# Attention stage of a four-stage block: the next batch's queries transposed between the scores of heads 1 and 2, their squares taken before the output copy, and the low parts of the key/value and output weights computed on GpSimd

## The reference, cut to what matters

```
q, k, v = projections of x[b]                 # 32 query heads, 8 key/value heads, D = 128
q, k = rope(rmsnorm(q)), rope(rmsnorm(k))
k_all = concat(cached keys (512), new k (128));  v_all likewise      # pages by block table
scores = q @ k_all.T * D**-0.5, masked where cache position >= cache_seqlens[b]
probs = softmax(scores);  o = probs @ v_all
x = x + o.reshape(S, 32*D) @ Wo.T             # then dense, SwiGLU and adapter stages on x
```

## Time and profile before

| what | value |
|---|---|
| median of 3 runs | 1509.14 us (1508.47 to 1510.86) |
| profiled execution | 1509.87 us, its span 1508.1 us |
| TensorE busy | 1410.0 us, 93% of the span |
| VectorE, ScalarE, GpSimd busy | 1023.3, 849.9, 667.3 us |
| granted TensorE clock, mean | 0.988 |

### The profile page before, as it was taken

One profiled execution on the slowest core, in us unless ns is written; L12 is line 12 of the kernel. 1 busy time (PEld: TensorE's weight loads), 2 busy tenths in 40 slices (PEclk: granted clock), 3 DMA queues, 4 the chain that ended last, 5 costly groups with the idle time before them and its releaser, 6 DMA issues. The chain is left out here.

```text
span 1508.1 us, 25464 instructions
## 1 busy us (share of the span) xinstructions
PE 1410.0 (93%) x7864; PEld 1211.3 (80%) x7864; DVE 1023.3 (68%) x2128; ACT 849.9 (56%) x2191; POOL 667.3 (44%) x971
## 2 busy tenths in 40 slices
PE   3799999999999999999999999999999796999998
PEld 2678888888888888788888878888888576888886
DVE  7666777777777777776777677777777454545543
ACT  3555665566666656665665566656656445434444
POOL 5788644444544544455454444544444280010112
PEclk9999999999999999999999999999999998999999
DMA  5243235414611561344135414522120344443422
GB/s 184 105 138 126 62 105 158 110 43 140 187 36 47 159 185 28 92 146 139 45 100 155 118 43 140 173 51 56 35 58 7 119 155 141 148 150 112 168 98 98
DMA packets 185182, 164.41 MB, mean 109 GB/s; under 512 B 122608, under 2 KB 159344, under 8 KB 174832
## 3 DMA queue, kind: packets, MB, share of 16 engines
q1 hardware_dynamic: 178352, 127.60, 28.4%
q0 software_dynamic: 6720, 35.66, 7.2%
HBM read 131.77 MB, written 31.46 MB: 108 GB/s over the span
## 5 line engine op out<-in xcount | busy, mean ns | idle before, releaser
L469 ACT ACTIVATE at_pT_hi<-at_ps 128x512 fp32r<-128x512 f32 x320 | 180.0, 599 | 193.9 <-PE at_ps L852 192.2
L636 DVE TENSOR_TENSOR at_pT_lo<-at_ps,at_pT_hi 128x512 fp32r<-128x512 f32 x320 | 209.9, 685 | 110.2 <-ACT at_pT_hi L469 109.8
L401 POOL TENSOR_SCALAR at_probs<-at_probs,at_row_inv 128x640 f32<-128x640 f32 x256 | 209.6, 821 | 157.1 <-DVE at_row_inv L687 151.7
L681 DVE CUSTOM_DVE_ANT_0 at_scores<-at_ps,at_mask,at_inv_rms 128x640 f32<-128x640 f32 x256 | 223.6, 877 | 73.7 <-PE at_ps L65 66.7
L512 ACT ACTIVATE at_probs<-at_scores,at_neg_max 128x640 f32<-128x640 f32 x256 | 213.1, 833 | 53.8 <-DVE at_neg_max L681 51.4
L63 PE MATMUL at_ps<-at_kT_hi,at_qT_hi 128*128 128x320 f32 x512 | 166.2, 325 | 25.8 <-DVE at_neg_max L681 23.2
L852 PE MATMUL at_ps<-ident,at_probs 128*128 128x128 f32 x1280 | 160.8, 273 | 1.8 <-POOL at_probs L401 1.8
L64 PE MATMUL at_ps<-at_kT_lo,at_qT_hi 128*128 128x320 f32 x512 | 159.1, 311 | 0.0
L65 PE MATMUL at_ps<-at_kT_hi,at_qT_lo 128*128 128x320 f32 x512 | 159.0, 311 | 0.0
L852 PEld LDWEIGHTS at_ps<-ident,at_probs 128*128 128x128 f32 x1280 | 145.4, 141 | 12.7 <-POOL at_probs L401 3.2
L63 PE MATMUL at_ps<-at_pT_hi,at_v_hi 128*128 128x512 f32 x320 | 134.1, 419 | 6.8 <-DVE at_pT_lo L636 6.8
(11 more groups left out here) (217 smaller groups left out, 3549.0 us busy)
## 6 DMA issues: line engine op xcount, KB each, us to landing
kT_pages<-at_kv_stage SPq DMA_DIRECT2D x14, 1024.0 KB
v_pages<-at_kv_stage SPq DMA_DIRECT2D x14, 1024.0 KB
at_k_raw<-kT_pages SPq DMA_DIRECT2D x56, 256.0 KB, 4.9
at_v_raw<-v_pages SPq DMA_DIRECT2D x56, 256.0 KB, 3.8
sw_wgu_raw<-in_sw_gu SPq DMA_DIRECT2D x22, 512.0 KB, 3.4
staging<-in_L_cond_Wq SPq DMA_DIRECT2D x8, 1024.0 KB, 5.4
staging<-in_L_cond_Wo SPq DMA_DIRECT2D x8, 1024.0 KB
ds_mask_raw<-in_mask_Bx4096x_ik SPq DMA_DIRECT2D x8, 1024.0 KB, 4.9
```

What stands on the lines that cost most here:

```text
L401: pool.tensor_scalar(probs[:, h, :], probs[:, h, :], row_inv[:, h:h + 1], 1.0, ALU.mult, ALU.mult).then_inc(probs_done, 1)
L469: act.activation(out, src, ACT.Copy).then_inc(done, 1)
L636: dve.tensor_tensor(out, src, hi_part.bitcast(F32), ALU.subtract).then_inc(done, 1)
L681: dve.tensor_tensor_reduce(out=scores[h % 2][:], in0=slot(h), in1=mask[:, b, :], scale=inv_rms[b % 2][:, h:h + 1], scalar=3.0e38, op0=ALU. ...
```

## The change

1. TensorE issues the next item's `queries` after the scores of head 1 in place of after those of head 3; `late_kv` is gone, so every item has `project_kv` before the transposes of the probabilities.
2. ScalarE takes `squares` one item earlier: at the end of an item, for the next but one, ahead of the output copy. The squares of (0, 1) stand before the first item.
3. The lo parts of the key/value weights (two instructions of 128x512 per group) and, but for group 0, those of Wo (four per group) are computed by GpSimd. The key/value weights move from b = 7 to b = 6, and the slots move: three query groups after the next item's cached keys, the fourth after two probability transposes, the key/value groups (and the second half of Wo) after the last one. The semaphore `wqkv_done` is split into `wq_done` and `wkv_done`; the load of Wo waits for the first alone.

```diff
             groups = {0: {2: [0, 1], 3: [2, 3]}}
             if not last:
-                groups[B - 2] = {0: [0], 1: [1], 2: [2], 3: [3]}
-                groups[B - 1] = {0: [4], 1: [5]}
+                groups[B - 2] = {0: [0, 1, 2], 1: [3], 3: [4, 5]}
             return groups.get(b, {}).get(slot, [])
+
+        def split_apart(first, b, n):
+
+            return n >= DC if b else not first
...
                         wait_apart(sp, wo_done, g * WO_GROUPS + WO_GROUPS, sp_passed)
+                        wait_apart(sp, wkv_done, g * KV_GROUPS + KV_GROUPS, sp_passed)
                         load_qkv(g + 1)
...
                     if not last and b == B - 1:
-                        wait_apart(sp, wqkv_done, g * QKV_GROUPS + 2 * QKV_GROUPS, sp_passed)
+                        wait_apart(sp, wq_done, g * DC + 2 * DC, sp_passed)
                         load_wo(g + 1)
...
+            def qkv_group(g, n):
+                cs = slice(2 * (n - DC), 2 * (n - DC) + 2)
+                wait_apart(pool, wqkv_hi_done, g * QKV_GROUPS + n + 1, pool_passed)
+                pool.tensor_tensor(wkvT_lo[:, cs, :], wkv_raw[:, cs, :], wkvT_hi[:, cs, :].bitcast(F32), ALU.subtract).then_inc(wkv_done, 1)
+
+            def wo_group(g, n):
+                wait_apart(pool, wo_hi_done, g * WO_GROUPS + n + 1, pool_passed)
+                pool.tensor_tensor(woT_lo[:, n, :], wo_raw[:, n, :], woT_hi[:, n, :].bitcast(F32), ALU.subtract).then_inc(wo_done, 1)
...
                         key_scale(g1, b1)
+                    if b == 0 and not first:
+                        wo_group(g, 0)
+                    if more:
                         rotate_k(g1, b1)
                     if by_row:
                         gather(b2, range(2), k_rows, k_raw, k_loaded)
+                    if b == 0 and not first:
+                        wo_group(g, 1)
+                        wo_group(g, 2)
+                    if b == B - 2 and not last:
+                        qkv_group(g + 1, DC)
+                        qkv_group(g + 1, DC + 1)
                     if more2:
                         rotate_q(g2, b2)
+                    if b == 0 and not first:
+                        wo_group(g, 3)
...
-                    if more:
-                        squares(g1, b1)
-                    exps(g, b, 0)
-                    exps(g, b, 1)
-                    weights(0)
-                    exps(g, b, 2)
-                    exps(g, b, 3)
+                    for h in range(G):
+                        exps(g, b, h)
                     if more:
                         queries(g1, b1)
-                    weights(1)
-                    if more:
                         cached_keys(g1, b1)
+                    weights(0)
                     probs_T(g, b, 0)
                     probs_T(g, b, 1)
-                    weights(2)
+                    weights(1)
                     if more:
                         cached_values(g1, b1)
                         new_kv(g1, b1)
                     probs_T(g, b, 2)
+                    weights(2)
                     probs_T(g, b, 3)
+                    probs_T(g, b, 4)
                     weights(3)
-                    probs_T(g, b, 4)
                     if more:
                         new_keys(g1, b1)
+                    if more2:
+                        squares(*following(g1, b1))
                     hi(oT_hi[:], bank(O_BANK), pv_done, upto(g, b, KC, KC), oT_hi_done)
...
                         for n in weight_groups(b, slot, last):
-                            if b < 2:
-                                wo_group(g, n)
-                            else:
-                                qkv_group(g + 1, n)
+                            if not split_apart(first, b, n):
+                                if b < 2:
+                                    wo_group(g, n)
+                                else:
+                                    qkv_group(g + 1, n)
...
-                    late_kv = b == B - 1 and not last
-                    for h in range(G):
-                        score(g, b, h)
+                    score(g, b, 0)
+                    score(g, b, 1)
                     if more:
                         queries(g1, b1)
+                    score(g, b, 2)
+                    score(g, b, 3)
                     if not (first and b == 0):
                         output(g, b, range(G))
-                    if late_kv:
-                        project_ahead(range(2))
-                    elif more:
+                    if more:
                         project_kv(g1, b1)
...
-                    if late_kv:
-                        project_kv(g1, b1)
-                    else:
-                        project_ahead(range(2))
+                    project_ahead(range(2))
```

More of the change, by code:

```diff
@@ L190, in attention @@
         wqkv_hi_done = sem("wqkv_hi_done")
-        wqkv_done = sem("wqkv_done")
+        wq_done = sem("wq_done")
+        wkv_done = sem("wkv_done")
         wo_hi_done = sem("wo_hi_done")
@@ L240, in attention @@
         sp_passed = sem("sp_passed")
-        QKV_GROUPS, WO_GROUPS = DC + DC // 2, G
+        KV_GROUPS, WO_GROUPS = DC // 2, G
+        QKV_GROUPS = DC + KV_GROUPS
         def xT_raw(b):
@@ L290, in _ @@
                     load_qkv(0)
-            sp.wait_ge(wqkv_done, QKV_GROUPS)
+            sp.wait_ge(wq_done, DC)
             load_wo(0)
@@ L535, in _ @@
             new_keys(0, 0)
+            squares(0, 1)
             def group(g, last):
@@ L539, in group @@
                     g1, b1 = following(g, b)
-                    more = not (last and b == B - 1)
+                    more, more2 = not (last and b == B - 1), not (last and b >= B - 2)
                     def weights(slot):
@@ L644, in qkv_group @@
                 out, src, h = (t[:, n, :] if n < DC else t[:, cs, :] for t in ((wqT_lo, wq_raw, wqT_hi) if n < DC else (wkvT_lo, wkv_raw, wkvT_hi)))
-                lo(out, src, h, wqkv_hi_done, g * QKV_GROUPS + n + 1, wqkv_done)
+                lo(out, src, h, wqkv_hi_done, g * QKV_GROUPS + n + 1, wq_done if n < DC else wkv_done)
             def wo_group(g, n):
@@ L804, in project_q @@
                     if b == 0:
-                        pe.wait_ge(wqkv_done, g * QKV_GROUPS + c + 1)
+                        pe.wait_ge(wq_done, g * DC + c + 1)
                     ins = three_pass(pe, bank(Q_BANK), xT_hi[:, c, at], xT_lo[:, c, at], wqT_hi[:, c, :], wqT_lo[:, c, :], c == 0, c == DC - 1)
@@ L812, in project_kv @@
                 if b == 0:
-                    pe.wait_ge(wqkv_done, g * QKV_GROUPS + QKV_GROUPS)
+                    pe.wait_ge(wkv_done, g * KV_GROUPS + KV_GROUPS)
                 for c in range(DC):
```

## The result

The changed kernel takes 1471.94 us (median of 4 runs, 1471.15 to 1473.14), the kernel before on the same chip 1510.0 us: ratio 0.9748, 95% interval 0.9731 to 0.9765. The forecast was 1478, its range 1471 to 1490. The profiled execution has a span of 1470.7 us against 1508.1, 37.4 less, where the sum of the prediction gave 31.4.

The account below looks back on a forecast made before the run. TensorE, busy 1410.0 of 1508.1 us, was taken as the bound, so its waits count. Gains 20.6 + 2.5 + 14.7 less 6.4 of new waits gave 31.4 us, hence 1478 us, range 1471 to 1490.

Parts of the forecast that it names:

- the new waits: TensorE waiting for keys and queries delayed by GpSimd's lo parts: 6.4 us lost, 0.5 of it for groups 1 and 7.
- Queries into the gap: TensorE transposes the next queries while waiting to start head 2: 20.6 us gained in groups 1 to 6, 2.5 in group 7.
- the rival of the rotation as the bound: TensorE's moved query transposes wait for GpSimd's rotation in every item: 10 us of gain lost, 1488 us; chance 0.15.
- the gap move: Rival: TensorE reaches the probabilities 0.43 earlier and waits there; 23.1 us lost, 1501 us; chance 0.05.
- Squares: ScalarE's squares before the output copy: cost nothing, covered by its 0.36 wait; otherwise at most 0.3 to 0.5 per item.
- Weights: Items 6, 7 and 0 shed weight work and waits: 0.71, 0.40 and 0.99 each, seven times, 14.7 us gained.
- GpSimd's lo parts: Each 128x512 weight lo part on GpSimd takes 1.29 us, with 2841 ns the other end.
- the rival of a held GpSimd: VectorE holds up GpSimd's lo parts, 1.55 us more each: 54 us lost, 1532 us; slower 0.04, near break-even 0.02, less 0.02.
- the strictest reading of that rival: Each GpSimd lo part held by one VectorE lo part of some 0.7 us: 24 us lost, 1502 us.
- and the 1.06 of the jump stay: In b = 0, head 2's 1.06 us delay after the loop's jump remains; only 0.99 of that item's excess goes.
- the item starts late: In groups 2 to 6, item 0's late start makes GpSimd's lo parts cost 0.9 each: 4.5 us of new waits.
- Group 0: Items of the group with GpSimd's gathers: 0.43 won, about 0.7 lost to the late queries' rotation; counted as zero overall.

Follow-up runs that it names:

- padded: Changed kernel with 14 increments of a semaphore nobody waits for inside VectorE's loop, which then lies at 337-708: 1476.6 us.
- shifted: Changed kernel with 14 idle semaphore increments ahead of VectorE's loop, moving it unchanged in length from 337-694 to 351-708: 1474.7 us.
- squares late: Changed kernel with ScalarE's squares back at the item's start, all else as changed: 1492.0 us.
- weights alone: Changed kernel with queries again after head 3's scores and squares at the item's start; weight lo parts stay on GpSimd: 1495.1 us.
- order alone: Kernel before with only queries and squares moved as in the change; all lo parts stay on VectorE in their old places: 1490.6 us.
- placed repaired kernel: Changed kernel with group 0 ordered as before, GpSimd rotating queries one lo part earlier, and 14 idle increments ahead of ScalarE's loop: 1467.8 us.
- kernel before, shifted: Kernel before with fewer doubled semaphore waits on VectorE, moving its loop from 339-708 to 315-684: 1524.0 us.

## Why the prediction was right, and where its terms were off

The direction, the range and the main mechanism held. That the time lies inside the range, 0.9 above its lower end, is in part luck. The prediction gave 1471 to 1472 a chance of 0.03 and meant by it that the new waits would be absent. About half of them are there; the time came so low because a stall went that the sum let stay and no rival priced as going, and a loss in group 0, not priced either, took about half of that back. The kernels that keep the stall, padded (1476.6) and shifted (1474.7), show what the forecast's own terms are worth: they lie 1.4 and 3.3 us below its 1478. By the prediction's own steps, from the profiled executions:

- Queries into the gap: 0.43 an item was forecast, and items 2 to 5 of groups 1 to 7 are 11.8 us shorter (0.43 x 24 + 0.36 x 4 = 11.8). The transposes start at 1.76, the margin of 0.05 against the rotation holds: the rival of the rotation as the bound does not occur, nor does the gap move. Group 7's items are 16.81, not 16.76.
- Squares: free, as forecast, but for more than was said. I costed the move at nothing and looked only at ordinary items. At the jump it covers most of ScalarE's 2 us. The run with the squares late prices it under the queries' move: 20 us, 6 of them by TensorE's clock. The squares' move by itself was not run.
- Weights: item 6 at 16.87 (0.71 gone, as forecast), item 7 at 17.07 with the forecast 0.2 of wait.
- GpSimd's lo parts: 1292 ns against 1.29 forecast; the rival of a held GpSimd (2841 ns) is refuted in all 42 of them (1282 to 1313 ns). Each operation of VectorE that ran beside one had an input in PSUM, as the prediction argued; none had two inputs in SBUF, so the strictest reading of that rival, 0.7 us a part, didn't come to a test.
- **The step that failed: "and the 1.06 of the jump stay".** I took the jump's stall for a fixed price of the jump. It was the fetch of VectorE's code, and the change, with 12 instructions fewer in VectorE's loop, happened to move the loop from 339-708 to 337-694. The padded and the shifted kernel, which change no work, put it back. Items 0 of groups 2 to 6 are 12.3 us shorter where I had 5 x 1.22 = 6.1; 5.1 of the difference is the jump.
- The term hung on it: "the item starts late" was the reason for 4.5 of the 6.4 us of new waits. The item starts in time, and item 1 waits 0.18 for the queries, not 0.7. Items 1 are 1.7 us shorter in sum; forecast was about 0.6 longer, the 0.5 for groups 1 and 7 not counted.
- Group 0 was counted as zero and is 2.2 us longer (158.46 against 156.24). In items 2, 3, 4 and 6 the queries wait 0.42 to 0.44 for a rotation that ends at 2.3, and the weight parts' new slots cost 0.6 in each of items 0, 1 and 6: with the weights alone group 0 loses 1.5, with the order alone 0.6. The row that showed the late rotation stood in the prediction; I let waits at the items' ends absorb it, and they did so only in part. The slots had no term at all.

From 31.4: 6.2 more in items 0, 2.3 more in items 1, the 0.5 added for groups 1 and 7 that no item shows, and 3.1 less in group 0 (where 0.9 had been counted as a gain) make 37.3 of the 37.4 measured.

What stays open: why a stalling loop takes five packets a turn and not four or six, and whether GpSimd's or TensorE's loops could be caught in the same way. In the placed repaired kernel no loop of any engine is fetched again in the two turns read; no run moved GpSimd's or TensorE's loop on purpose.

## What to carry to other kernels

Idle time of an engine right behind a loop's jump, with instruction packets in the DMA queues beside it, was code being fetched here; suspect it there: count the packets over one turn, and try a few idle instructions ahead of the loop before any work is moved. Look at every engine's loop at once: the kernel before with VectorE's loop placed well and ScalarE's worse than it lay was 3.4 us slower than with neither placed. A kernel change can alter such a stall by accident, here by 1 to 2 us a turn, so compare variants with that queue's count beside the time, and put work that doesn't depend on the new turn ahead of the jump. And where one engine serves two order changes, price them together: here the squares' place looked free in every ordinary item and was worth 20 us under the queries' move. And before a longer item is put down to waits, read its granted clock: 6 of those 20 us were 3.4 us at half clock in four items.

## What the runs showed of the hardware

The loops that were not fetched again lay on VectorE at 327-696, 337-694 and 339-696, on ScalarE at 244-511. Those that were lay on VectorE at 337-708, 339-708, 351-708 and, with a second wait, 315-684; on ScalarE at 226-492, 230-497 and, with a second wait, 240-506. Theory F (three pieces of 128) fits VectorE but not ScalarE: an edge at 241 to 244 puts 226-492 into three pieces, and it stalls. What fits all eleven is this, formed afterwards and not tested on a new kernel: pages of 256 instructions with an edge at 316 to 324 on VectorE and 241 to 244 on ScalarE, two of them held, and the next one fetched in place of the older when the second half of a page is entered. A loop then stays only if it starts behind an edge and ends less than 384 instructions further. The Trainium skill ("Runtime: NRT & Kernel Launch", "Instruction fetch mechanics") gives the page's size and the two pages; the eleven places fit both, though no run measures either by itself. That half a page is the trigger is my reading of the runs. The stall lengthened item 0 by 1.0 to 1.3 us a turn when VectorE's loop had it. ScalarE was idle for about 2 us, and for 1.6 more where a second wait came within a few instructions.

TensorE's granted clock is 1.00 throughout the loop in before and in the changed kernel. With the squares late it fell to 0.50 for 3.4 us in four of five items 0, after waits of 2.1 us in that item; in the kernel before, shifted, in two of five, after waits of 1.4 to 1.6 and of 1.0 us. Each fall cost about 1.5 us.
